# Eight stacked layers on one core: attentions with per-head exponents, 32-column values, 64-partition score tiles and a new order of work

## The reference, cut to what matters

```python
for h in range(16):                       # attention 0: head width 64; attentions 1 and 3: width 8
    s = q_h @ k_h.T / sqrt(width)         # 0: causal and padding mask; 1: padding mask; 3: no mask, but biases
    out_h = softmax(s) @ v_h
x += tanh(g) * (concat(out_h) @ Wo.T + b)
```

## Time and profile before

| what | value |
|---|---|
| runs | 553.59 to 556.07 us, median 554.44 us |
| span of the profiled execution (first to last instruction) | 552.6 us |
| median of the runs less that span | 1.8 us |
| TensorE matmul busy | 449.9 us, 81% of the span |
| VectorE, ScalarE, GpSimd busy | 347.0, 267.4 and 205.6 us |
| 28 to 158 us: first attention, from step 4 with F0 | TensorE busy 121.5 of 130.1 us |
| 158 to 286 us: F0 and ROUTE with A1 | TensorE busy 114.3 of 127.2 us |
| 305 to 351 us: MOE | TensorE busy 41.8 of 46.2 us |
| 411 to 516 us: A3 with F2, then with F3 | TensorE busy 94.1 of 104.9 us |

### The profile page before, as it was taken

One profiled execution on the slowest core, in us unless ns is written; L12 is line 12 of the kernel. 1 busy time (PEld: TensorE's weight loads), 2 busy tenths in 40 slices (PEclk: granted clock), 3 DMA queues, 4 the chain that ended last, 5 costly groups with the idle time before them and its releaser, 6 DMA issues.

```text
span 552.6 us, 8568 instructions
## 1 busy us (share of the span) xinstructions
PE 449.9 (81%) x2862; PEld 358.3 (65%) x2862; DVE 347.0 (63%) x1001; ACT 267.4 (48%) x525; POOL 205.6 (37%) x370
## 2 busy tenths in 40 slices
PE   5789899999998789889993799356769999988842
PEld 3478788797786566667782599243546776766621
DVE  1167776977977777768774021355547668789773
ACT  3355435564555245445541233034576766666552
POOL 6071010110122444338726000375256546565351
PEclk9999999999999798989995699857879999999755
DMA  8960000000000030000001241110000000000000
GB/s 355 387 230 1 1 1 1 2 1 0 1 2 1 0 117 1 0 1 11 15 14 35 85 140 38 40 38 21 0 0 1 2 1 1 2 0 1 2 0 39
DMA packets 7131, 21.95 MB, mean 40 GB/s; under 512 B 1216, under 2 KB 3505, under 8 KB 6705
## 3 DMA queue, kind: packets, MB, share of 16 engines
q1 hardware_dynamic: 6065, 19.31, 9.6%
q0 software_dynamic: 1024, 2.10, 1.3%
HBM read 14.52 MB, written 6.88 MB: 39 GB/s over the span
## 4 chain that ended last, share of the span: by engine, by line
PE 55%; DVE 18%; ACT 8%; POOL 8%; issue 7%; DMA 3%; SPq 0%; DVEq 0%; POOLq 0%; ACTq 0%
PE bank L759 6%; PE bank L767 5%; PE bank L784 5%; PE bank L801 5%; PE bank L754 4%; PE bank L924 4%; PE bank L780 4%; PE bank L915 3%; PE bank L796 3%; DVE prob L1126 2%; PE bank L747 2%; POOL rstd L443 2%; DMA pack<-pack_d 2%; PE bank L890 2%; POOL kz L474 2%
## 5 line engine op out<-in xcount | busy, mean ns | idle before, releaser
L441 POOL TENSOR_SCALAR rstd<-mv 128x1 f32<-128x1 f32 x64 | 13.2, 206 | 238.4 <-DVE mv L1080 236.2
L1120 DVE TENSOR_REDUCE mx<-bank 128x4 f32<-128x512 f32 x96 | 66.0, 688 | 46.6 <-PE bank L759 29.6
L527 ACT ACTIVATE prob<-prob 128x512 f32<-128x512 f32 x96 | 60.1, 626 | 41.2 <-DVE prob L1126 40.7
L474 POOL TENSOR_TENSOR kz<-kT,pack 128x256 f32<-128x256 f32 x128 | 77.7, 641 | 0.0
L519 ACT ACTIVATE probT<-bank 128x512 f32<-128x512 f32 (+1 forms) x104 | 58.9, 567 | 38.9 <-PE bank L767 38.2
L767 PEld LDWEIGHTS bank<-pack,prob 128*128 128x128 f32 x384 | 48.0, 144 | 36.2 <-issue 26.7
L759 PE MATMUL bank<-kz,qT 128*128 128x512 f32 x128 | 69.7, 628 | 0.1
L1126 DVE TENSOR_TENSOR prob<-bank,mx 128x512 f32<-128x512 f32 x96 | 65.0, 677 | 2.3 <-PE bank L767 1.4
L784 PEld LDWEIGHTS bank<-va,probT 128*128 128x128 f32 x512 | 63.9, 196 | 0.7 <-ACT probT L519 0.7
L784 PE MATMUL bank<-va,probT 128*128 128x9 f32 x512 | 62.8, 250 | 0.4 <-ACT probT L519 0.4
L767 PE MATMUL bank<-pack,prob 128*128 128x128 f32 x384 | 59.5, 278 | 2.8 <-ACT hid L617 1.3
(11 more groups left out here) (213 smaller groups left out, 925.7 us busy)
## 6 DMA issues: line engine op xcount, KB each, us to landing
yrows_d<-moe_rows SPq DMA_DIRECT2D x2, 1510.0 KB, 20.6
pack<-pack_d SPq DMA_DIRECT2D x1, 2112.0 KB, 15.2
expert<-experts_d SPq DMA_DIRECT2D x4, 514.0 KB, 9.4
pack<-experts_d SPq DMA_DIRECT2D x4, 514.0 KB, 4.3
pack<-pack_d SPq DMA_DIRECT2D x1, 2048.0 KB, 9.8
xrows_d<-moe_rows SPq DMA_DIRECT2D x1, 1080.0 KB, 18.9
moe_rows<-xrows_d SPq DMA_DIRECT2D x8, 135.0 KB, 3.1
yrows_d<-o_n SPq DMA_DIRECT2D x8, 135.0 KB, 1.8
```

The lines of the kernel that those rows point to most:

```text
L474: pool.tensor_tensor(kz[:, it.k, P * h:P * h + 2 * P].rearrange("p (h t) -> p h t", h=2), kT[:, bass.ds(it.b, 1), :].to_broadcast([P, 2, P ...
L527: act.activation(prob[:, g % 2, :], prob[:, g % 2, :], ACT.Exp, scale=float(DK0 if layer == A0 else DK) ** -0.5).then_inc(E[layer]["probs" ...
L1120: yield from do(dve.tensor_reduce(m, src, AX.X, ALU.max))
```

## The change

- Keys of A1 and A3: computed by `k4` and masked while they leave PSUM, by ScalarE and VectorE in halves (`k4_sb`, 4 instructions each for the whole layer), into `kz4`, which serves all four groups. For A1 this happens ahead of the steps, for A3 after the last step of ROUTE. GpSimd's `mask_keys` and the `kz` buffers are gone. The query is spread over `qz` instead: four evacuations of 32 partitions each (`q_sb`).
- Exponent: `top_of` on VectorE gives only the negated maxima; `exps` on ScalarE reads the score bank and does one activation for each head with the maximum as its bias. The score bank is free after the fourth.
- Values of A1 and A3: computed item by item (`v`, `v_sb`), in blocks of 32 columns in `vz`. `pv` now has these 32 columns as the stationary operand and the transposed probabilities as the moving one, with outputs on partitions 32j to 32j+31; four more matmuls with `sumsel` give the sums on the same partitions. The result comes out transposed, so `ot` and `ot_sb` are gone in A1 and A3, and `norm` takes the reciprocal of 128 x 128 sums.
- A0: keys are evacuated as they are (`k0`), and `scores0` makes two groups at once with contractions over 64 partitions, alternating between the upper and the lower half and between the two score banks.
- Layer norm: GpSimd does the subtraction and product too (`rs`), except for F0 and F3, where the quantization is computed from x minus mean and the root is folded in later.
- F0 and F3: less on ScalarE, products straight from PSUM, GpSimd's `weigh` gone (`gate0`, `hid0`, `square3`, `hq3`, `sumsq3`).
- The lists of slots are new for nearly every layer; A0 is one step shorter, A2 one step longer.

The core of the diff:

```diff
-LAG = [3, 2, 3, 1, 2, 3, 2, 3, 2]
+LAG = [2, 2, 3, 1, 2, 4, 2, 3, 2]
...
+            pool.memset(qz[:, :, :, :], 0.0).then_inc(cleared, 1)
+            pool.memset(vz[:, :, :], 0.0).then_inc(cleared, 1)
...
+                z, k = SIDE[layer], it.k
+                ev = E[layer]["rs"]
+                wait(pool, layer, "ln", it)
+                if it.rep == 0 and layer == A0:
+                    pool.wait_ge(pool_const, 1)
+                scale, eps = (1.0 + RMS_EPS, RMS_EPS * LN_EPS) if layer == F3 else (1.0, LN_EPS)
+                inverse_root(rstd[z][:, k, 0:1], mv[z][:, k, 1:2], scale, eps, ev, it, 1)
+                if layer in (F0, F3):
+                    return
+                if it.rep >= 2:
+                    wait(pool, layer, "xt", it.back(2))
+                elif layer in PREVIOUS:
+                    wait(pool, PREVIOUS[layer], "xt", Item(B - 2 + k, B - 2 + k))
+                pool.wait_ge(ev.sem, ev.at(it, 2))
+                out = xn_all[:, it.b, :] if layer == ROUTE else xn[z][:, k, :]
+                pool.tensor_scalar(out, x_sb[:, it.b, :], mv[z][:, k, 0:1], rstd[z][:, k, 0:1], ALU.subtract, ALU.mult).then_inc(ev.sem, 1)
...
-            def mask_keys(it, layer, kT, half):
-                if it.rep == 0 and half == 0:
-                    pool.wait_ge(kv_act, 2 if layer == A1 else 6)
-
-                if it.rep >= 2:
-                    wait(pool, layer, "scores", it.back(2))
-                elif layer == A1:
-                    wait(pool, A0, "scores", Item(B - 2 + it.k, B - 2 + it.k))
-                for h in range(H // 2 * half, H // 2 * half + H // 2, 2):
-                    pool.tensor_tensor(kz[:, it.k, P * h:P * h + 2 * P].rearrange("p (h t) -> p h t", h=2),
-                                       kT[:, bass.ds(it.b, 1), :].to_broadcast([P, 2, P]),
-                                       col["hmask"][:, h:h + 2].rearrange("p (h a) -> p h a", a=1).to_broadcast([P, 2, P]),
-                                       ALU.mult).then_inc(E[layer]["kz"].sem, 1)
...
             def exps(it, layer, g):
-                wait(act, layer, "shifted", it, 2 * g + 2)
-                act.activation(prob[:, g % 2, :], prob[:, g % 2, :], ACT.Exp,
-                               scale=float(DK0 if layer == A0 else DK) ** -0.5).then_inc(E[layer]["probs"].sem, 1)
+                wait(act, layer, "max", it, g + 1)
+                if g >= 2 or it.rep >= 1:
+                    wait(act, layer, "probsT", it, g - 1)
+                elif layer == A1:
+                    wait(act, A0, "probsT", Item(B - 1, B - 1), g + 3)
+                elif layer == A3:
+                    wait(act, A2, "probsT", Item(B - 2 + g, B - 2 + g))
+                for j in range(GH):
+                    act.activation(prob[:, g % 2, P * j:P * j + P], bank[S_BANK[g % 2]][:, P * j:P * j + P], ACT.Exp,
+                                   bias=mx[:, g % 2, j:j + 1]).then_inc(E[layer]["probs"].sem, 1)
 
...
             def k_sb(it, c):
                 wait(act, A0, "kps", it, c + 1)
-                kv = kz[:, it.k, :].rearrange("p (t a n) -> p t a n", t=8, a=2)
-                src = bank[R_BANK[0]][:, :].rearrange("p (t n) -> p t n", t=4)
-                for a in range(2):
-                    evac(kv[64 * a:64 * a + 64, 4 * c:4 * c + 4, a, :], src[64 * a:64 * a + 64], A0, "k_sb")
+                evac(k0[:, it.k, 512 * c:512 * c + 512], bank[R_BANK[0]][:, :], A0, "k_sb")
...
             def q_sb(it, layer):
                 wait(act, layer, "q", it)
-                if layer == A3:
-                    evac(qT[:, it.k, 0:P], bank[R_BANK[1]][:, 0:P], layer, "q_sb", bias=col["bq_3"])
-                else:
-                    evac(qT[:, it.k, 0:P], bank[R_BANK[1]][:, 0:P], layer, "q_sb")
+                for g in range(G):
+                    rows = slice(32 * g, 32 * g + 32)
+                    kw = dict(bias=col["bq_3"][rows]) if layer == A3 else {}
+                    evac(qz[rows, it.k, g, :], bank[R_BANK[1]][rows, 0:P], layer, "q_sb", **kw)
+
+            def v_sb(it, layer):
+                wait(act, layer, "v", it)
+                wait(act, layer, "pv", it.back(2))
+                into = vz[:, it.k, :].rearrange("p (g n) -> p g n", g=G)[:, :, 0:P].rearrange("p g (j n) -> p g j n", j=GH)[:, :, :, 0:DK]
+                evac(into, bank[R_BANK[0]][:, 0:P].rearrange("p (g j d) -> p g j d", g=G, j=GH), layer, "v_sb")
 
...
+            def k4_sb(n, c):
+
+                act.wait_ge(k4_pe, 2 * n + c + 1)
+                for j in range(GH):
+                    kw = dict(bias=bk_s[:, j:j + 1]) if n else {}
+                    act.activation(kz4[:, 4 * c:4 * c + 4, j, :], bank[K4_BANK[n][c]][:, :].rearrange("p (b t) -> p b t", b=4),
+                                   ACT.Identity, scale=col["hmask"][:, j:j + 1], **kw).then_inc(k4_act, 1)
...
-                    [(3, ot_sb, layer), (1, exps, layer, 0), (2, probsT_sb, layer, 3)],
+                    [(1, exps, layer, 0), None, (2, probsT_sb, layer, 3)],
                     [(1, exps, layer, 1), (1, probsT_sb, layer, 0), (0, xt_sb, layer)],
-                    [(1, exps, layer, 2), (1, probsT_sb, layer, 1), (0, q_sb, layer)]]
+                    [(1, exps, layer, 2), (1, probsT_sb, layer, 1), (0, q_sb, layer), (0, v_sb, layer)]]
...
+            def scores0(it, c):
+                for a in range(2):
+                    mask_scores(it, A0, 2 * c + a)
+                wait(pe, A0, "q_sb", it, 1 + c)
+                wait(pe, A0, "k_sb", it, 1 + c)
+                for i in range(GH):
+                    t = slice(P * (GH * c + i), P * (GH * c + i) + P)
+                    for a in range(2):
+                        rows = slice(DK0 * a, DK0 * a + DK0)
+                        mm_ = pe.matmul(bank[S_BANK[a]][:, P * i:P * i + P], qT[rows, it.k, t], k0[rows, it.k, t],
+                                        start=False, stop=(i == GH - 1))
+                        if i == GH - 1:
+                            mm_.then_inc(E[A0]["scores"].sem, 1)
...
+                wait(pe, layer, "q_sb", it, g + 1)
+                if it.rep == 0 and g == 0:
+                    pe.wait_ge(k4_act, 4 if layer == A1 else 8)
+                    pe.wait_ge(k4_dve, 4 if layer == A1 else 8)
+                pe.matmul(bank[S_BANK[g % 2]][:, :].rearrange("p (h t) -> p h t", h=GH), qz[:, it.k, g, :], kz4[:, it.b, :, :],
+                          start=layer != A1, stop=True).then_inc(E[layer]["scores"].sem, 1)
...
-                    else:
-                        va = va_1 if layer == A1 else va_3
-                        mm_ = pe.matmul(bank[O_BANK[it.k]][:, VW * h:VW * h + VW], probT[:, g % 2, P * j:P * j + P],
-                                        va[:, bass.ds(it.b, 1), h, :], start=True, stop=True)
+                    pe.matmul(out[QW * j:QW * j + QW, 0:P], vz[:, it.k, QW * h:QW * h + QW], probT[:, g % 2, P * j:P * j + P],
+                              start=(g == 0), stop=(g == G - 1), skip_group_check=True)
+                for j in range(GH):
+                    mm_ = pe.matmul(out[QW * j:QW * j + QW, P:2 * P], col["sumsel"][:, QW * g:QW * g + QW], probT[:, g % 2, P * j:P * j + P],
+                                    start=False, stop=(g == G - 1), skip_group_check=True)
                 mm_.then_inc(E[layer]["pv"].sem, 1)
 
...
+            def v(it, layer):
+                claim(it, layer, "v")
+                n = 0 if layer == A1 else P
+                pe.matmul(bank[R_BANK[0]][:, 0:P], ctxT[:, it.b, :], col["wvT_13"][:, n:n + P], start=True, stop=True
+                          ).then_inc(E[layer]["v"].sem, 1)
...
-                    [(1, scores, layer, 0), (2, probsT, layer, 2), (2, pv, layer, 1), (3, ot, layer)],
-                    [(1, scores, layer, 1), (2, probsT, layer, 3), (2, pv, layer, 2), (3, y, layer)],
-                    [(1, scores, layer, 2), (1, probsT, layer, 0), (2, pv, layer, 3), (0, xt, layer)],
-                    [(1, scores, layer, 3), (1, probsT, layer, 1), (0, q, layer), (1, pv, layer, 0)]]
+                    [(1, scores, layer, 0), (2, probsT, layer, 2), (2, pv, layer, 1)],
+                    [(3, y, layer), None, (1, scores, layer, 1), (2, probsT, layer, 3), (2, pv, layer, 2)],
+                    [(1, scores, layer, 2), (1, probsT, layer, 0), (0, xt, layer), (2, pv, layer, 3)],
+                    [(1, scores, layer, 3), (1, probsT, layer, 1), (0, q, layer), (0, v, layer), (1, pv, layer, 0)]]
...
-                A0: [[(1, scores, A0, 0), (2, probsT, A0, 2), (3, ot0, 1), (2, pv, A0, 1), (0, proj0, "k", 0), (0, kv3, 0)],
-                     [(1, scores, A0, 1), (2, probsT, A0, 3), (0, proj0, "k", 1), (3, y0), (2, pv, A0, 2), (0, xt, A0),
-                      (2, ot0, 0), (0, kv3, 1)],
-                     [(1, scores, A0, 2), (1, probsT, A0, 0), (0, proj0, "v", 0), (0, proj0, "q", 0), (2, pv, A0, 3), (0, kv3, 2)],
```

(57 more changed lines are left out.)

634 lines of the change are left out of this document (345 added, 289 removed).

## The result

The changed kernel takes 579.9 us (median of 4 runs, 578.8 to 581.8) against 555.3 for the kernel before: 1.042 times as long, 95% interval 1.036 to 1.048. The forecast was 533, the range ended at 565.

What follows compares the result with a forecast made beforehand. TensorE was taken to bound A0 with F0 and A1 with ROUTE, other stages being mixed or chains. Terms -8 - 10.9 + 14.8 - 6 - 5 - 1 + 2 - 7 = -21.1 gave 533 us, range 497 to 565.

Steps and rivals of the forecast that it cites:

- The frame: Whole prediction: called wrong if tile-form switches cost more than 0.16 us or a new wait in A0 opens gaps.
- a new order that stalls: A0 or A2: the new order stalls them; the remaining case, chance 0.04.
- Scores in A0: TensorE in A0: a pair of groups costs 1.04 us instead of 1.74, 16 pairs, -10.9 us.
- Values: `pv` in A1 and A3: a group costs 1.04 us instead of 0.81, 64 groups, +14.8 us in all.
- the first rival: Narrow matmuls: all four quarters run at once, a values group costs 0.51 us with switches; 505 us, chance 0.32.
- Start: Before A0's first scores: key and value work of A3 and halved evacuations go, -8 us, first scores near 20 us.
- VectorE and GpSimd: TensorE's waits for these engines shrink: -6 us in F0 with A1, -5 in A3 with F3, -1 in A0.
- ScalarE, +2: A3 with F2: four exponents a group instead of one fill ScalarE; collisions cost +2 us.
- the third rival: A3 with F2: TensorE waits for a score bank through gelu's table loads, 3 us a step; +14, 547 us, chance 0.13.
- End, -7: F3's last items: fewer operations behind the root and a shorter hidden part, -7 us.
- A2, 0: A2 with longer lag and new order: no change, between -8 and +6 us.
- No overlap, 587: Narrow matmuls run one after another, a values group costs 1.79 us; +32.3, 587 us, chance 0.13.

Runs made afterwards that it cites:

- all six moves: Changed kernel with weights, output projection, `places`, `v` matmul, `v_sb` and ROUTE's `xt_sb` moved in the lists: 544.7 us, ratio 0.979.
- the order mended: Changed kernel with three moves (weights behind the copy of oT, output projection before the second q projection, `places` late): 551.4 us, ratio 0.989.
- without the loads: Third feed-forward's gelu left out, and its table loads with it: 538.8 us for the changed kernel with six list moves, 550.0 for the kernel before.

## Why the prediction was wrong

**The frame.** "The prediction is wrong in its frame ... if a new wait in A0 opens gaps where TensorE had none": this happened, in A0 and in A1 with ROUTE, and a new order that stalls had a chance of 0.04. The step that failed is the one before the sum: the new lists were in the diff, and I priced operations only, with the order taken as neutral. Each of the three spots could be read from the diff by the questions that the forecast put to other moves: what stands behind `(0, weights)` on VectorE, who waits for it (`ot_sb0`, and through the bank the q projection), which piece held the bank before `y0`, and what `places` waits for. They cost 10, 5 and 10 us alone and 29 together, the order of `v` and `q` with ROUTE's copy another 6: 35 of the 47 us between forecast and result. But the forecast also holds an error the other way, some 20 us on the values (below). With the values as measured the same sum would have said about 513, so the order explains 35 of some 67 us. The largest piece of what is left is A0: 150.6 us with all six moves where 146.4 - 10.9 - 1 = 134.5 were forecast.

**Scores in A0, -10.9.** The price was right (1.04 forecast, 1.10 measured, and 1.64 without alternation), the assumption "16 pairs on the path" wrong. That the price fits says little for its argument, nine passes because the two passes of a matmul follow each other: for the values the same argument fails. Measured worth: nothing in the changed kernel, 4 us with the order mended. A stage in which TensorE was busy for 95% of the time is bound by TensorE only as long as its work isn't cut: with 0.64 us less a pair it waited for other engines. Which of their latencies rules these steps is not shown.

**Values, +14.8.** Wrong in sign, and the first rival had the sign right. TensorE's timeline of the changed kernel, a group in A1 in which nothing waits:

```profile
287.95 0.63 PE L811 MATMUL bank<-pack,prob 128*128 128x128 f32 x4
288.52 0.43 PE L832 MATMUL bank<-probT,vz 128*32 128x128 f32 x8
288.76 0.40 PE L835 MATMUL bank<-probT,pack 128*32 128x128 f32 x8
289.09 0.49 PE L895 MATMUL bank<-pack 128*128 128x128 f32 x2
```

From 288.52 to 289.09 the group takes 0.57 us; without their switches, rival 1 said 0.43 and I 0.96. The transposes ahead of it take 0.57 here and most often 0.53, where they took 0.44; ahead of the 65 columns of A0 they still take 0.44. So the switch costs 0.09 to 0.13. Together that is 0.66 to 0.70 instead of 0.81: 64 groups give -7 to -10 us, not +14.7, and the whole term -5 to -7 instead of +14.8. The argument "the second pass needs the same quarter, so eight matmuls take nine passes" is refuted: they take 5.3. The estimate from the Trainium skill ("TensorE: Matmul & The Clock Gate", Measured speedup vs the span model), 0.72 us, was far nearer than mine, and "TensorEngine Tiling (Array Packing)" (Key Properties) is borne out on both of its points, tiles that run in parallel and a cost for the change of form. (The prediction took 0.28 us a group and 16 us from that estimate; with its own two switches it is 1.04 - 0.80 = 0.24 and 14 us. A0's terms in the first two rivals are 16 x 0.80 = 12.8 and 16 x 0.05 = 0.8 where 12.5 and 1.3 stand. None of this changes what was forecast.)

**Start, -8.** Measured -3.5, first scores at 24.8 instead of "near 20". The removed work stood where TensorE waits for its first weights: up to 12.2 us the kernel before has it busy for 5.9 us, the changed kernel for 3.8. Then comes:

```profile
12.54 2.08 PE L852 MATMUL bank<-pack 128*128 128x128 f32 x8 [2.78 <-DMA pack<-pack_d]
15.30 2.07 PE L852 MATMUL bank<-pack 128*128 128x128 f32 x8 [0.69 <-ACT k L535]
...
18.96 2.07 PE L847 MATMUL bank<-pack 128*128 128x512 f32 x2 [0.37 <-ACT xnT L535]
...
23.25 1.15 PE L852 MATMUL bank<-xnT,pack 128*128 128x128 f32 x8
```

The eight passes of a projection last 2.08 us up to about 22 us and 1.15 after it, where the kernel before has 1.16 us for the same eight passes already at 12.23. The length is that of the eight passes at 77.43 (2.05 us), where the granted clock is 0.50. But here, from 12.50 to 22.00 us, the profile gives a granted clock of 1.00, so that the clock is the cause is not shown. The five operations from 12.54 on (2.08, 2.07, 0.45 for the transpose at 18.15, 2.07 and 1.72 for the q projection at 20.83) take 8.4 us, and the same forms later 4.8 (1.15, 1.15, 0.28, 1.02 and 1.15), so 3.6 us of the missing 4.5 are here. Why they are slow there, and whether the removed work would mend it, no run tested.

**VectorE and GpSimd, -12 in all.** A3 with F3 went as forecast (-4.3; I had -5). The half of 12.9 us in A1 with F0 gave -2.9, with 5.9 us of waits for the copy of `v`; with these mended the stretch is 59.4 us instead of 68.4. The reciprocal takes 0.948 us (0.90 forecast), GpSimd's row 0.80 to 1.02 (0.3 to 0.7 forecast), and moving that back to VectorE changes nothing that can be told.

**ScalarE, +2, and the third rival, +14.** The four exponents take 1.14 us (1.1 forecast). TensorE is idle for 10.5 us in four steps of A3 with F2, 2.6 a step, over the 2 that I had named as the sign of a collision; the stretch is +5.5 where my own terms (+2, and a quarter of the values' +14.8) give +5.7. The sum agrees for a wrong reason: the values gained. The rival's wait is real (1.16 us), and without the loads the changed order gains 1.5 us a step where the kernel before gains 0.5. So its mechanism is likely, and about 1 us a step stands against its price of 3. My remark that the bank's longer hold "is covered" failed exactly where the rival said, behind the table load.

**End, -7.** -4.5. From the transpose of the last item's row (537.90 before, 564.86 after) to the first transposes of its hidden row F3 takes 6.1 us instead of 8.7; the rest is not taken apart. **A2, 0:** +2.4, of which 2.3 was `places`.

**No overlap, 587.** Its time is nearest to the result, and its mechanism is false; only the distance between two starts, not the total, could tell. That 580 lies near 587 is chance.

## What to carry to other kernels

A reordering is a change of its own, and it deserves a sum of its own: for each entry that moved, list what is now queued behind it on its engine and which piece held its bank before. A saving on an engine that is 95% busy counts in full only if the next latency is far away; look for the second bound before multiplying by the count. Two traces can be compared stretch by stretch only where the granted clock is the same: one step at 0.80 hid that the table loads weigh three times as much in the changed attention. And a kernel that comes out slower after many edits may hold a faster one: one entry moved at a time, where the timeline shows a bracket, turned 1.042 into 0.979.

## What the runs showed of the hardware

Four 32-column tiles overlap in float32, two passes a matmul: eight matmuls over 128 columns took 0.57 us where one after another would be 16 x 0.107 = 1.71, and it doesn't matter whether neighbours write the same 32 partitions in pairs (0.60) or not (0.57). The two 64-row halves overlap only when their matmuls alternate (1.10 us for eight) and not in runs of four (1.64). Entering the 32-column form cost 0.09 to 0.13 us. ScalarE's copy with bias of 32 partitions by 128 columns (0.36 us; 0.26 without bias) costs nearly as much as its exponent with bias over 128 partitions by 128 columns (0.38). Each table load took 1.28 us, and exponents that read a score bank behind it made TensorE wait for the bank for 1.05 to 1.16 us.
